# A graph layer with a mixture of experts: two node chunks per edge group, and edge writes ordered only where receivers can overlap

## The reference, cut to what matters

```python
x = x + gnn(layernorm(x), edge_attr_3, edge_attr_8, ..., (src, dst))
x = x + ffn(layernorm(x)[None], ...)[0]

# gnn, per edge:  s, v = 64 scalars and 64 x 3 vectors of the sender's normalised row
sh1 = sqrt(3) * edge_vectors / (norm(edge_vectors) + 1e-9)
w   = (silu(emb @ fc_w1 / sqrt(8)) @ fc_w2 / sqrt(64)).reshape(-1, 5, 64)
m0  = (w0 * s + w3 * dot(v, sh1) / sqrt(3)) / sqrt(2)
m1  = (w1 * s * sh1 + w2 * v + w4 * cross(v, sh1) / sqrt(2)) / sqrt(3)
agg = segment_sum(m, receiver) / 16
out = agg @ lin / sqrt(64) + layernorm(x)
```

## Time and profile before

| | us |
|---|---|
| median of 3 runs (1460.46 to 1460.99) | 1460.74 |
| profiled execution | 1463.16 |
| its span | 1461.4 |
| PE / DVE / ACT / POOL busy | 1216.7 / 1001.6 / 955.3 / 1014.3 |
| first stage, until SP loads for routing | 386.5 |
| first edge write of POOL starts | 124.8 |

### The profile page before, as it was taken

How to read it: one execution, slowest core, us unless ns; L and a number is a source line. 1 busy time by engine, 2 the same in 40 slices (tenths; PEclk the granted TensorE clock), 3 DMA queues, 4 the chain that set the end, 5 groups by cost and what they waited for, 6 DMA issues and landing times.

```text
span 1461.4 us, 26674 instructions
## 1 busy us (share of the span) xinstructions
PE 1216.7 (83%) x7872; PEld 1076.8 (74%) x7872; DVE 1001.6 (69%) x2132; ACT 955.3 (65%) x2128; POOL 1014.3 (69%) x918
## 2 busy tenths in 40 slices
PE   2434688998499532999999999999999999999993
PEld 0222355555365232999999999999999999999993
DVE  7889979998299894755756655755755565556653
ACT  4788977776166552766667766667766676657662
POOL 6886787676477403667777767777776777778785
PEclk9966788889799776999999999999999999999996
DMA  9999945444567302433433422343522343233333
GB/s 328 286 332 341 261 90 74 67 70 55 128 218 217 133 10 79 102 47 44 109 43 52 111 44 43 63 90 49 111 47 43 48 108 51 43 48 55 51 53 42
DMA packets 131625, 152.97 MB, mean 105 GB/s; under 512 B 17034, under 2 KB 118474, under 8 KB 131422
## 3 DMA queue, kind: packets, MB, share of 16 engines
q0 software_dynamic: 51456, 64.07, 27.9%
q1 hardware_dynamic: 58446, 66.59, 14.0%
q10 hardware_dynamic: 21648, 21.45, 4.3%
HBM read 98.79 MB, written 53.28 MB: 104 GB/s over the span
## 4 chain that ended last, share of the span: by engine, by line
PE 54%; issue 3%; POOL 2%; ACT 1%; DMA 1%; DVE 0%; ACTq 0%; POOLq 0%; DVEq 0%
PE f_ps_y L1545 26%; PE f_ps_h L1533 25%; PE f_ps_x L1523 2%; POOL out L1424 1%; POOL xg L1406 1%; POOL sg L1410 0%; DMA sg<-stat_rows,idx_row 0%; ACT h_all L1473 0%; ACT h_hi L1472 0%; ACT y_all L1483 0%; ACT f_xn L1457 0%; DMA out<-clean,put_now 0%; DMA sg<-stat_rows,idx_now 0%; DVE clean L1610 0%; DVE x_lo L1578 0%
## 5 line engine op out<-in xcount | busy, mean ns | idle before, releaser
L1472 ACT ACTIVATE h_hi<-f_ps_h,c_b 128x384 fp32r<-128x384 f32 (+1 forms) x416 | 236.8, 569 | 264.7 <-PE f_ps_h L1533 264.7
L1583 DVE TENSOR_TENSOR h_lo<-h_all,h_hi 128x768 fp32r<-128x768 f32 (+1 forms) x208 | 184.3, 886 | 256.6 <-ACT h_all L1473 256.0
L1545 PE MATMUL f_ps_y<-w_hi,h_hi 128*128 128x256 f32 x1136 | 324.9, 286 | 0.0
L1545 PE MATMUL f_ps_y<-w_lo,h_hi 128*128 128x256 f32 x1136 | 319.8, 282 | 0.0
L1545 PE MATMUL f_ps_y<-w_hi,h_lo 128*128 128x256 f32 x1136 | 319.7, 281 | 0.0
L1424 POOL DMA_INDIRECT out<-clean,put_now x159 | 261.9, 1647 | 57.6 <-issue 50.0
L1406 POOL DMA_INDIRECT xg<-out,idx_now x159 | 191.9, 1207 | 129.2 <-issue 118.7
L1533 PE MATMUL f_ps_h<-x_hi,w_hi 128*128 128x384 f32 (+1 forms) x832 | 272.1, 327 | 8.0 <-issue 3.5
L1533 PE MATMUL f_ps_h<-x_lo,w_hi 128*128 128x384 f32 (+1 forms) x832 | 269.7, 324 | 0.0
L1533 PE MATMUL f_ps_h<-x_hi,w_lo 128*128 128x384 f32 (+1 forms) x832 | 269.4, 324 | 0.0
L1473 ACT ACTIVATE h_all<-f_ps_h,c_b 128x384 f32<-128x384 f32 (+1 forms) x416 | 237.7, 571 | 0.0
(11 more groups left out here) (212 smaller groups left out, 2288.9 us busy)
## 6 DMA issues: line engine op xcount, KB each, us to landing
shared<-out SPq DMA_DIRECT2D x40, 512.0 KB, 3.4
w_raw<-in_w SPq DMA_DIRECT2D x16, 1024.0 KB, 5.3
xin<-in_x SPq DMA_DIRECT2D x24, 512.0 KB, 7.3
out<-xin ACTq DMA_DIRECT2D x24, 512.0 KB, 5.6
shared<-in_x SPq DMA_DIRECT2D x16, 512.0 KB, 5.6
out<-shared ACTq DMA_DIRECT2D x16, 512.0 KB, 5.1
dst_row<-in_dst SPq DMA_DIRECT2D x20, 256.0 KB, 3.8
xg<-out,idx_now POOLq DMA_INDIRECT x159
```

The costliest lines, as they stand in the source:

```text
L1472: nc.scalar.activation(h_hi[:, f, :n * P], ps_h[:, f % SLOTS, :n * P], ACT.Relu, bias=b1[:, e, f:f + 1])
L1545: ins = nc.tensor.matmul(ps_y[:, i], x[:, f, i * P:(i + 1) * P], weights[s][:, w], start=i != 1 and f == 0 and n == 0, stop=f == KF - 1 an ...
L1583: tt(h_lo[:, pair, :n * P], h_all[j % 2][:, :, :n * P], h_hi[:, pair, :n * P].bitcast(F32), ALU.subtract).then_inc(h_lo_ready, 1)
```

## The change

Only the first stage is changed.

- STEPS is 10: the first ten groups run with two chunks each (DVE in steps 0 to 7, for chunks 4 to 19), the last ten alone. DVE takes edge statistics and coefficients ahead by a rule (`statistics_step`, `coefs_step`): two groups a step at first, then up to six groups ahead. The small edge tiles get eight buffers (AHEAD), not four. Six late gathers stand behind the writes of groups 5, 6 and 7. BY_POOL is 7, so DVE takes four batches' roots, not three.
- PE: `radial_first` stands ahead of `aggregate`, not behind it. `radial_second` of the next group waits for `w_taken`, when DVE has read ps_w for the last time; DVE's message instructions are reordered for this.
- ACT: `radial_hidden` stands at the start of a group, half of the directions ahead of `take_agg` and half behind it.
- Writes: two semaphores by parity of the group. A group waits for the writes of the group before the last, and for those of the last group only if its smallest receiver is not above that one's largest. DVE computes this from the groups' ends, which go through DRAM as `chunks` did; POOL reads the number to wait for from `writes_needed`. The trash rows are doubled, so that neighbouring groups use different ones.

```diff
-    STEPS = 5
+    STEPS = 10
+    AHEAD = 8
-    BY_POOL = 8
+    BY_POOL = 7
...
@@ gpsimd, scatter(g) and the program
-                pool.wait_ge(scattered, 64 * g + 64)
+                pool.wait_ge(scattered[g % 2], 64 * (g // 2) + 64)
+                if g == 0:
+                    pool.wait_ge(scattered[1], 64)
+                else:
+                    landed = pool.value_load(writes_needed[0:1, g:g + 1], min_val=64, max_val=32 * EG + 64)
+                    pool.wait_ge(scattered[(g - 1) % 2], landed)
+                    pool.sem_inc(spare_pool, 1)
...
             for n in range(3, BY_POOL):
+                gather(2 * n - 1)
+                gather(2 * n)
                 node_scales(n)
-                for g in (2 * n - 1, 2 * n):
-                    if g < SLOTS:
-                        gather(g)
-                if n % 2:
-                    edge_scales(n // 2 + 2)
+                edge_scales(2 * n - 3)
+                if 2 * n - 2 < STEPS:
+                    edge_scales(2 * n - 2)
+            gather(2 * BY_POOL - 1)
             pool.wait_ge(chunks_known, 16)
+            pool.wait_ge(writes_known, 1)
             for g in range(EG):
                 scatter(g)
-                if STEPS <= g + 4 < EG - 1:
-                    edge_scales(g + 5)
-                if 1 <= g < 4:
-                    gather(SLOTS + 2 * g - 2)
-                    gather(SLOTS + 2 * g - 1)
+                if STEPS <= g + 7 < EG:
+                    edge_scales(g + 7)
+                if 5 <= g < 8:
+                    gather(SLOTS + 2 * (g - 5))
+                    gather(SLOTS + 2 * (g - 5) + 1)
...
@@ scalar, the loop over groups
+                add_own_rows(2 * g)
+                radial_hidden(g + 1)
...
+                next_rows(g + 1)
+                rows_by_direction(g + 1, (0, 1))
                 take_agg(g - 1)
+                if g + 1 < STEPS:
+                    add_own_rows(2 * g + 1)
+                rows_by_direction(g + 1, (2, 3))
                 take_upd(g - 1)
...
@@ tensor
-                    pe.wait_ge(msg_ready, g)
+                    pe.wait_ge(w_taken, g)
...
@@ vector, messages
-                chain.mark(tt(tmp_g[:], tmp_b[:], tmp_c[:], ALU.add))
-                chain.wait(2)
-                chain.mark(tt(vec(tmp_h), vec(tmp_a), w3(4), ALU.mult))
+                chain.wait(1)
+                tt(vec(tmp_h), vec(tmp_a), w3(4), ALU.mult).then_inc(w_taken, 1)
+                chain.mark(tt(tmp_g[:], tmp_b[:], tmp_c[:], ALU.add))
...
@@ vector, step(g)
+                if g + 2 < STEPS:
+                    messages(g, 2 * g + 4)
+                    node_coefs(BATCH[2 * g + 2])
+                    node_statistics(2 * g + 5)
...
+            def statistics_step(n):
+                return (n - 3) // 2 if n < STEPS else n - 6
+
+            def coefs_step(n):
+                if n < 2:
+                    return -1
+                return (n - 1) // 2 if n < STEPS else n - 2
+
+            def overlapping_writes():
+                constants.wait(v)
+                v.wait_ge(ends_known, 32)
+                chain.link(tt(overlap[:, 1:], lasts[:, :EG - 1], firsts[:, 1:], ALU.is_ge))
+                nc.vector.scalar_tensor_tensor(out=writes_needed[:, 1:], in0=overlap[:, 1:], scalar=64.0,
+                                               in1=constants["write_counts"][:, 1:], op0=ALU.mult,
+                                               op1=ALU.add).then_inc(writes_known, 1)
```

154 lines of the change are left out of this document (78 added, 76 removed).

## The result

| | before | changed |
|---|---|---|
| median of 5 runs, us | 1460.99 | 1450.94 |
| lowest to highest | 1460.46 to 1464.6 | 1446.74 to 1453.49 |
| profiled execution (span) | 1463.16 (1461.4) | 1453.49 (1451.7) |

The ratio is 0.9915 (95% interval 0.9895 to 0.9935): 10.1 us faster by the medians. The forecast was 1447.4 in a range of 1436 to 1459. Two repeats of the changed kernel, each beside runs of the kernel before on its own chip, gave 0.9924 (0.991 to 0.9938) and 0.9897 (0.9876 to 0.9919).

What follows compares the result with a forecast made beforehand. POOL, with DMA beside it, bound the first stretch; DVE and PE with waits the second. Messages 19 11.1 us earlier plus 2.2 at the tail is 13.3 us: 1449.9 beside the profile, 1447.4 beside the median; range 1436 to 1459.

Steps and rivals of the forecast that it cites:

- The mixed stretch: Eight steps with two chunks each, paced by DVE: 175.5 us plus 5 us of waits, step 9 at 217.5.
- rival (b): Ring of six chunk buffers or ACT paces the two-chunk steps: 20.5 to 22 us each, total 1463, no gain; chance 0.10.
- The edge-only stretch: Ten intervals, messages 9 to 19, paced by the loop through PE and ACT: 12.5 us each, 125 us, ending at 344.8.
- close under DVE: ACT's work per two-chunk step, about 18.5 us with waits, beside DVE's 18.5 to 20.2; it was to hide.
- the rest is 0.7 us each: Excess per edge-only interval over 13 old intervals, added to the 11.8 us loop to give 12.5 us.
- Rival (a): Edge-only loop slows as PE takes more low-clock passes: gain gone at 13.8 us per interval, 1472 at 15; chance 0.11.
- The writes: POOL's writes, 7.7 us a group from near 127 us: 15 landing waits go, giving room to catch up and 2.2 us.
- the prediction's list: Group borders sharing a receiver, where POOL still waits for landings: 4 of 19, before groups 4, 5, 8 and 18.
- With 15 old waits it wouldn't: Claim that POOL catches up before the end, but not with 15 old landing waits of up to 4 us.
- rival (d): Landing waits stay or POOL never catches up: POOL ends near 400 us, total 1474; chance 0.03.
- The tail: Last group's update copy to its write: 2.7 us wait goes, less some 0.5 for loading the count, 2.2 us gained.
- What counted nothing: Overlap test, three small SP DMAs, more trash rows, one more tensor_reduce: under 1 us each, counted as nothing, bounds 0 and 3.

Runs made afterwards that it cites:

- stores at once: Changed kernel with SP's embedding and receiver loads early, ACT's chunks 18 and 19 behind group 10's rows, chunk 17's second half stored immediately: 1498.24 us, ratio 0.994.

## Why the prediction was right, point by point

**The mixed stretch.** From the first step to step 9 it took 176.2 us (38.30 to 214.48). DVE's own work was put at 175.5, which is right to 1 us, and 5 us for waits, of which 1.5 came; the start was 1.3 us later than the 37 taken. POOL, ACT and DMA hid behind DVE as argued, and rival (b) didn't occur. Step 9 came 3.0 us before the forecast. (Rival (b) gives 1463 us as 1447.4 plus its 16, but 5 of these are in 1447.4 already; its own numbers make 1458.)

**The edge-only stretch: the term that was mis-sized.** Ten intervals of 12.5 us were forecast, as one size, from the mean of the kernel before. They took 127.6 us, 12.76 each, so the sum is near; but it consists of 45.9 us for three and 81.7 for seven, 11.7 each. The loop is faster than the forecast where it is alone, since the low clock that was carried over from before nearly left it (0.98 against 0.91 from 260 to 344 us), and the hand-over, which has no term in the sum, costs 11 us over steady pace. The steps that failed are two. The line on ACT ("close under DVE") was read for the steps in the middle, and not for the last one, where DVE stops having chunks and ACT has two left; PE waits for it, at the low clock before and after. Between executions, up to 7 of those 11 us go with the clock, and some 4 stay at the highest clock seen there. And "the rest is 0.7 us each" took the low-clock passes of the old order for a property of the kernel: with the old order put back, 12 to 19 takes 86.5 us again, with the new one 80.7 to 83.2. The loop was computed as equally long, 11.9 and 11.4 us, and what the order gives over seven intervals, 4 us by the means of the kernels with the old and the new order (85.9 and 81.9), comes with the higher clock. It comes from the order and not from the writes: with all old landing waits and the new order the seven take 81.5 us, with the new writes and the old order 84.9 and 86.5. That the sum is right to 0.4 us (messages 19 start at 344.41, forecast 344.8) is luck: messages 9 come 3.0 us early, the hand-over takes 8.4 us more than its three intervals of 12.5, and the seven behind it 5.8 us less. Part of it is the luck of one execution too: the repeats have messages 19 at 339.7 and 341.9.

**Rival (a)** was the clock falling further. It did so in the hand-over (0.78 from messages 9 to 12, before 0.83), and behind it the clock rose to 0.98; over 192 to 356 us it is 0.88, before 0.89. The mean of 12.76 us an interval stayed far from the 13.8 at which the rival had the gain gone. The Trainium skill (TensorE: Matmul & The Clock Gate, Part 1: The HAM clock gate) says that activity lifts the throttle; rows agree up to the hand-over's end, where it is 0.70 to 0.81 and PE has its longest waits (6.88 us for an embedding at 156.23, 5.82 in the hand-over), but the prediction's use of it, that a reordered loop must be less dense, has no row for it.

**w_taken** was said to give nothing where the loop leads. In steady state DVE waits 1.5 us for ps_w, so the loop leads there; the edit wasn't tried alone.

**The writes.** The first write started at 127.03, forecast 127. Waits over 2 us that the profile gives to a landing stand ahead of groups 4, 5, 14 and 18. Three are shared borders of the prediction's list. The fourth, group 14, is none: its write starts 1.4 us behind the copy of its own update (ACT first, then POOL), the distance of the last group, so POOL waited for that update.

```profile
307.81 1.19 ACT L516 COPY xin<-ps_agg 128x768 f32<-128x768 f32 x1
```

```profile
310.42 1.55 POOL L418 DMA_INDIRECT out<-xin,upd_row  x1 [3.02 <-DMA out<-rows,upd_row]
```

POOL does catch up, then, from group 14 on, and stands free for 3.9 us ahead of groups 15, 16 and 17. "With 15 old waits it wouldn't" is shown by the kernel with the old waits, 1473.26 against the 1474 of rival (d); its writes end sooner than the rival's 400 us (SP's loads are at 394.44), and the 2.5 us in front of routing, below, bring it near. My first theory in the expectation for that kernel had dropped this argument of the prediction, and it fell.

**The tail.** From messages 19 to SP's loads are 29.3 us, before 30.6: 1.3 gained, forecast 2.2. The write starts 1.4 us behind the copy; how much of that is the load of its count, put at 0.5, no row shows.

**What counted nothing.** Two things were not foreseen. PE waited for embeddings, 11.5 us in three places up to 200 us, since SP's queue stood at a chunk's store; this lay in PE's slack, for with SP's loads early messages 9 start at 215.7, no earlier than in the repeats. The other counts: 2.5 us between SP's loads and routing. That distance is 7.67 to 7.69 us in all twelve profiled executions with ten steps, 5.2 before, 5.4 with the new writes alone. So it comes with the program and not from the writes; which part of it is open. By this 13.3 forecast minus 2.5 leaves 10.8, and 9.7 was measured between the profiled executions.

## What to carry to other kernels

Where two kinds of work run at different ratios on several engines, give the step in which one kind ends a term of its own: the engine that is ahead stops, and the engine behind has the rest before it. Check a wait that looks harmless against the pace after the change, not the pace before: the landing waits cost nothing that could be measured while groups came every 31 and then 12.6 us, and 23 us once they came every 20 and then 11.5. And if a wait changes its name under each repair and the sum stays, stop reordering: count the work, and compare the granted clock and the durations of the same matmuls between executions before naming a cause.

## What the runs showed of the hardware

- Groups of four accumulating indirect writes of 128 rows, each group waiting for the last one's landing, follow each other every 11.0 us here, with 1.55 us per write and 3.7 us or more from issue to landing (median 4.2 in that kernel). The Trainium skill (DMA: Bandwidth & Descriptors, Rules for kernel authors) has a second accumulation into the same bytes wait for the first one's semaphore; the runs show the price of waiting everywhere, 1473.26 against 1450.38 us.
- Seven passes with the same matmuls took 86.5 us in the old order, with the clock at 0.88, and 81.7 us in the new one at 0.98 (260 to 344 us). Two executions of one program differ as well: from messages 9 to 12 the changed kernel had 0.78 and 45.9 us, its first repeat 0.87 and 41.9 us.
- One chip ran the kernel before in 1506.9 us, 3% above the 1461 to 1463 of the others. Nearly all of it lies behind the first stage: the kernel with stores at once has SP's loads at 374.5 us there, the changed kernel at 373.7 on its chip, and the whole executions are 1503.55 and 1453.49 us. What sets this chip apart isn't shown.
